# Cross-attention with image tokens: scores in two 64-row halves, six PSUM banks, and the order of the softmax around them

## The reference

```python
q = _split_heads(hidden_states @ w_q, HEADS)
k = _split_heads(text @ w_k, HEADS)
v = _split_heads(text @ w_v, HEADS)
out_text = _merge_heads(_sdpa(q, k, v))            # 56 keys
mask_ip = _ip_mask(bbox, B, S, hidden_states.dtype)
k_ip = _split_heads(ip_h @ w_k_ip, HEADS)
v_ip = _split_heads(ip_h @ w_v_ip, HEADS)
out_ip = _merge_heads(_sdpa(q, k_ip, v_ip, mask=mask_ip))   # 8 keys
out = (out_text + out_ip) @ w_out + b_out + residual
```

## Time and profile before

| | |
|---|---|
| median of 3 runs | 881.37 us |
| lowest, highest | 880.84 us, 883.45 us |
| the profiled execution | 881.16 us, of which 879.4 us are its span |
| PE busy | 874.3 us, 99% of the span, 4716 matmuls |
| PE weight loads | 752.0 us, 86%, 4716 loads |
| DVE, ACT, POOL busy | 82%, 67%, 60% |
| DMA | 21% of 16 engines' span |

### The profile page before, as it was taken

The page is one execution under the profiler, slowest core; times in us unless marked ns, Lnnn a source line. Parts: engine busy times, 40 slices in busy tenths (PEclk is TensorE's granted clock), DMA queues, the critical chain, the costliest instruction groups (busy, mean ns, idle before and its releaser), DMA issues.

```text
span 879.4 us, 13951 instructions
## 1 busy us (share of the span) xinstructions
PE 874.3 (99%) x4716; PEld 752.0 (86%) x4716; DVE 723.2 (82%) x1017; ACT 591.2 (67%) x986; POOL 524.3 (60%) x421
## 2 busy tenths in 40 slices
PE   9999999999999999999999999999999999999998
PEld 8899888888888888888888888888888888888877
DVE  6779889797888879797887879787897978888785
ACT  7766685857767585765768486675858577574773
POOL 1059677392846649293755739375664929466581
PEclk9999999999999999999999999999999999999999
DMA  9924223011030403003030301204030210301011
GB/s 315 358 100 135 83 76 127 1 68 68 1 127 1 134 0 106 21 2 132 0 127 0 134 0 37 90 0 134 0 127 0 76 58 0 119 23 39 1 48 72
DMA packets 34203, 64.63 MB, mean 73 GB/s; under 512 B 4480, under 2 KB 6784, under 8 KB 34048
## 3 DMA queue, kind: packets, MB, share of 16 engines
q1 hardware_dynamic: 33888, 62.84, 21.1%
q10 hardware_dynamic: 288, 1.44, 0.4%
HBM read 40.34 MB, written 23.59 MB: 73 GB/s over the span
## 4 chain that ended last, share of the span: by engine, by line
PE 97%; DVE 2%; POOL 1%; ACT 1%; issue 0%; POOLq 0%
PE bank L95 25%; PE bank L97 25%; PE bank L96 25%; PE bank L1131 8%; PE bank L1151 4%; PE bank L1152 4%; PE bank L1040 1%; PE bank L1046 1%; PE bank L1043 1%; DVE total L225 1%; PE bank L1061 1%; PE bank L1058 1%; PE bank L1093 0%; DVE top L219 0%; PE bank L1083 0%; POOL prob L178 0%
## 5 line engine op out<-in xcount | busy, mean ns | idle before, releaser
L512 POOL TENSOR_TENSOR oT_lo<-o_raw,oT_hi 128x512 fp32r<-128x512 f32 x78 | 101.1, 1296 | 226.0 <-ACT oT_hi L681 225.9
L178 POOL TENSOR_TENSOR prob<-prob,top 128x1120 f32<-128x1120 f32 x126 | 177.7, 1440 | 0.0
L184 POOL TENSOR_TENSOR prob<-prob,inv 128x1120 f32<-128x1120 f32 x126 | 177.2, 1441 | 0.0
L95 PE MATMUL bank<-xT_hi,wq_hi 128*128 128x512 f32 x400 | 162.9, 407 | 0.0
L919 DVE TENSOR_TENSOR o_raw<-bank,pv_part 64x512 f32<-64x512 f32 x160 | 110.2, 689 | 62.6 <-ACT pv_part L677 60.1
L95 PE MATMUL bank<-oT_hi,wo_hi 128*128 128x512 f32 (+1 forms) x405 | 157.4, 389 | 0.0
L96 PE MATMUL bank<-oT_lo,wo_hi 128*128 128x512 f32 (+1 forms) x405 | 156.7, 387 | 0.0
L97 PE MATMUL bank<-oT_hi,wo_lo 128*128 128x512 f32 (+1 forms) x405 | 156.6, 387 | 0.0
L97 PE MATMUL bank<-xT_hi,wq_lo 128*128 128x512 f32 x400 | 156.5, 391 | 0.0
L96 PE MATMUL bank<-xT_lo,wq_hi 128*128 128x512 f32 x400 | 155.9, 390 | 0.0
L677 ACT ACTIVATE pv_part<-bank 64x512 f32<-64x512 f32 x160 | 94.9, 593 | 62.7 <-PE bank L1152 60.1
(11 more groups left out here) (121 smaller groups left out, 1695.2 us busy)
## 6 DMA issues: line engine op xcount, KB each, us to landing
xin<-in_xT SPq DMA_DIRECT2D x16, 1280.0 KB, 6.8
outT<-res SPq DMA_DIRECT2D x79, 256.0 KB, 6.8
w_raw<-in_L_xattn_w_k SPq DMA_DIRECT2D x8, 320.0 KB, 5.4
w_raw<-in_L_xattn_w_k_ip SPq DMA_DIRECT2D x8, 320.0 KB, 5.8
w_raw<-in_L_xattn_w_v_ip SPq DMA_DIRECT2D x8, 320.0 KB, 3.6
w_raw<-in_L_xattn_w_v SPq DMA_DIRECT2D x8, 320.0 KB, 3.5
v_raw<-v_scratch SPq DMA_DIRECT2D x14, 140.0 KB
prob<-in_textT SPq DMA_DIRECT2D x8, 224.0 KB, 5.0
```

What stands on the lines that cost most here:

```text
L95: nc.tensor.matmul(dst, a_hi, b_hi, start=first, stop=False)
L178: ins = eng.tensor_tensor(s, s, top[:, t, n, :].unsqueeze(2).broadcast_to([P, HEADS, k1 - k0]), ALU.subtract)
L184: ins = eng.tensor_tensor(s, s, inv[:, t, n, :].unsqueeze(2).broadcast_to([P, HEADS, k1 - k0]), ALU.mult)
L512: nc.gpsimd.tensor_tensor(oT_lo[:, m, :], o_raw[:, m % 2, :], oT_hi[:, m, :].bitcast(F32), ALU.subtract).then_inc(oT_lo_done, 1)
```

## The change

The keys of a block are no longer block-diagonal over 128 rows. `k_parts` holds, for each block and part, 128 columns in which rows 0 to 63 have heads 0 and 1 and rows 64 to 127 heads 2 and 3. A step becomes six matmuls of 64 rows and 128 columns instead of three of 128 rows and 256 columns: for each of the three products one with rows 0 to 63 and one with rows 64 to 127, in turn, and into different banks. Four steps fill two banks. Scores have six banks (0 to 5) instead of four; a pair of units waits until the pair three before it is copied, and units 4 and 5 wait for the last `pv_added` of the group before. The copies read a bank as 4 by 128 columns and write them into `prob` 256 columns apart. Where a tile needed 3, 5, 8 and 10 units copied, it now needs 4, 6, 8 and 10.

The fifth remainder of the attention output goes from POOL to the head of DVE's softmax. POOL subtracts maxima 0 before mask 2 and maxima 1 before mask 3. The first transposes go tile by tile for both pairs. In the setup, `text_values` waits for all ten copies where it waited for eight.

```diff
-        k_hi, k_lo = sb("k_hi", [P, KD, HPT, KEYS], F32R), sb("k_lo", [P, KD, HPT, KEYS], F32R)
+        k_parts = sb("k_parts", [P, KD, 2, PW], F32R)
...
-        s_bank, t_bank, v_bank = bank[0:4], bank[2:4], bank[4:6]
+        s_bank, t_bank, v_bank = bank[0:6], bank[2:4], bank[4:6]
...
-            return -(-(t + 1) * SW // 512)
+            return 2 * -(-(t + 1) * KD // RUN)
...
+        def score_dst(n):
+            steps = prob[:, n // 2 * RUN * CW:(n // 2 + 1) * RUN * CW].rearrange("p (i r c) -> p r i c", r=2, c=PW)
+            return steps[:, n % 2, :, :]
...
-            for half in range(2):
-                t, m = divmod(2 * n + half, KD)
...
-                keys = [k[:, m, :, :].rearrange("p j k -> p (j k)") for k in (k_hi, k_lo)]
-                ins = three(s_bank[n % 4][:, half * CW:(half + 1) * CW], qT_hi[:, m, q_cols], qT_lo[:, m, q_cols], *keys, True, True)
-            ins.then_inc(score_ready, 1)
+            if u == 0:
+                wait(pe, score_copied, UNITS * g)
+            elif u == 1:
+                wait(pe, pT_lo_done, PAIRS * g)
+            elif u == 2:
+                wait(pe, pv_added, PAIRS * g)
+            else:
+                pe.wait_ge(score_copied, UNITS * g + 2 * u - 4)
...
+            for i in range(RUN):
+                t, m = divmod(RUN * u + i, KD)
...
+                for n, (q, part) in enumerate(((qT_hi, 0), (qT_hi, 1), (qT_lo, 0))):
+                    for r in range(2):
+                        rows = slice(r * HP, (r + 1) * HP)
+                        ins = nc.tensor.matmul(s_bank[(2 * u + r) % 6][:, i * PW:(i + 1) * PW], q[rows, m, q_cols], k_parts[rows, m, part, :], start=n == 0, stop=n == 2)
+                        if i == RUN - 1 and n == 2:
+                            ins.then_inc(score_ready, 1)
...
                 def softmax(g):
                     add_mask(pool, g, 0)
-                    oT_part(g - 1, KD - 1)
                     add_mask(pool, g, 1)
-                    add_mask(pool, g, 2)
                     for t in range(GT):
                         sub_max(pool, g, t, 1)
-                        if t == 0:
-                            add_mask(pool, g, 3)
+                        if t < 2:
+                            add_mask(pool, g, t + 2)
...
+                def last_oT_part(g):
+                    dve.wait_ge(oT_lo_done, KD * g + KD - 1)
+                    dve.wait_ge(oT_hi_done, KD * (g + 1))
+                    nc.vector.tensor_tensor(oT_lo[:, KD - 1, :], o_raw[:, (KD - 1) % 2, :], oT_hi[:, KD - 1, :].bitcast(F32), ALU.subtract).then_inc(oT_lo_done, 1)
...
-                            pe.wait_ge(score_copied, UNITS if n == 0 else UNITS - 2)
+                            pe.wait_ge(score_copied, UNITS)
...
-                    p_transpose(g, 0)
-                    p_transpose(g, 1)
+                    pe.wait_ge(score_copied, UNITS * (g + 1))
+                    for t in range(GT):
+                        pe.wait_ge(prob_done, GT * g + t + 1)
+                        for p in range(2):
+                            ins = transpose_tile(g, p, t)
+                            if t == GT - 1:
+                                ins.then_inc(pT_ready, 1)
```

More of the change, by code:

```diff
@@ L40, in attention_kernel @@
     CW = HPT * KEYS
+    PW = 2 * KEYS
+    RUN = 512 // PW
     SW = HEADS * KEYS
@@ L127, in q_lo_part, with k_head @@
             nc.vector.tensor_tensor(qT_lo[:, m, :], l_bank[(m + 1) % 2][:], qT_hi[:, m, :].bitcast(F32), ALU.subtract).then_inc(q_lo_done, 1)
-        def k_head(t, j):
-            return t[j * DH:(j + 1) * DH, :, j, :]
+        def k_head(part, j):
+            return k_parts[j * DH:(j + 1) * DH, :, part, j % 2 * KEYS:(j % 2 + 1) * KEYS]
         def k_hi_part(act, b, raw=None):
@@ L136, in k_hi_part @@
             for j in range(HPT):
-                nc.scalar.activation(k_head(k_hi, j), raw[j * DH:(j + 1) * DH], ACT.Copy).then_inc(k_hi_built, 1)
+                nc.scalar.activation(k_head(0, j), raw[j * DH:(j + 1) * DH], ACT.Copy).then_inc(k_hi_built, 1)
         def k_lo_part(dve, b, raw=None):
@@ L200, in score_unit, with copy_scores @@
                 q_cols = slice(t * P, (t + 1) * P)
[L201 to L207 removed]
+                for n, (q, part) in enumerate(((qT_hi, 0), (qT_hi, 1), (qT_lo, 0))):
[4 more added lines that the diff above has]
+                            ins.then_inc(score_ready, 1)
+        def copy_scores(act, g, n):
+            act.wait_ge(score_ready, UNITS * g + n + 1)
+            nc.scalar.activation(score_dst(n), s_bank[n % 6][:].rearrange("p (i c) -> p i c", c=PW), ACT.Copy).then_inc(score_copied, 1)
         def exponentials(act, g, t, shared):
@@ L481, in _ @@
                                         pattern=[[-1, P]], channel_multiplier=1).then_inc(ident_made, 1)
-                for buf in (k_hi, k_lo):
-                    nc.gpsimd.memset(buf[:].rearrange("p m j k -> p (m j k)").bitcast(F32), 0.0).then_inc(k_zeroed, 1)
+                nc.gpsimd.memset(k_parts[:].rearrange("p m s c -> p (m s c)").bitcast(F32), 0.0).then_inc(k_zeroed, 1)
                 mine = pool_chunks
@@ L1113, in _ @@
                         ins.then_inc(k_ipT_ready, 1)
-                for n in range(UNITS):
-                    score_unit(pe, 0, n, 0, True)
+                for u in range(UNITS // 2):
+                    score_units(pe, 0, u, 0, True)
                 for k in range(KC):
@@ L1133, in p_transpose @@
                 def p_transpose(g, p):
-                    if p < 2:
-                        pe.wait_ge(score_copied, UNITS * (g + 1))
-                    else:
-                        pe.wait_ge(pT_lo_done, PAIRS * g + p - 1)
+                    pe.wait_ge(pT_lo_done, PAIRS * g + p - 1)
                     for t in range(GT):
-                        if p == 0:
-                            pe.wait_ge(prob_done, GT * g + t + 1)
                         ins = transpose_tile(g, p, t)
@@ L1192, in scores @@
                 def scores(g, b, new_batch):
-                    for n in range(UNITS):
-                        score_unit(pe, g, n, b, new_batch)
+                    for u in range(UNITS // 2):
+                        score_units(pe, g, u, b, new_batch)
                     for m in range(KD):
@@ L1215, in last_group @@
                 def last_group(g, b):
-                    for n in range(UNITS):
-                        score_unit(pe, g, n, b, False)
+                    for u in range(UNITS // 2):
+                        score_units(pe, g, u, b, False)
                     for m in range(KD - 1):
```

18 lines of the change are left out of this document (7 added, 11 removed).

## The result

The kernel after takes 922.92 us (919.37 to 923.34) beside 881.37 us (880.84 to 883.45) before: a ratio of 1.0459, with a 95% interval of 1.0448 to 1.0470. It is 4.6% slower, and the prediction of 879.8 us was wrong; so was its whole range, which ended at 896.

What follows compares the result with a forecast made beforehand. PE, busy for 99% of the span, was taken as the bound; -8.3 (pairs) + 5.4 (passages) + 0.9 (group 0) + 0.6 (last group) = -1.4 us took the profiled 881.16 us to 879.8, range 848 to 896.

Steps and rivals of the forecast that it cites:

- The pair of halves: Score stage: the two 64-row halves load weights side by side, 0.112 us a pair, -8.3 us in all; chance 45%.
- Short loads: Score stage: the half-size matmul shortens its load too, 0.062 to 0.067 us a pair, 852 us in all; chance 27%.
- the serial rival: Score stage: only one weight load runs at a time, 0.224 us a pair, 986 us in all; chance 12%.
- The passage: Each score stage: going into and out of 64-row work costs 0.34 us, +5.4 us over 16 stages.
- Group 0 and the last group: Group 0: PE waits for all ten copies, +0.9 us; last group: subtraction 0 starts later, +0.6 us.
- Third pair of banks, unit 6, the remainder: Score stage: bank and copy waits stay hidden, the banks' with 0.7 us left; DVE's 0.7 us remainder fits its idle time.
- POOL: Middle groups' softmax: mask 0 at 4.35 us, subtraction 0 at 6.45, POOL done at 29.95, PE arriving at 30.9.
- Masks later and transposes tile by tile: Softmax and first transposes: these edits move no PE work and gain nothing while POOL has slack, put at 0.9 us.
- My sign of being wrong: PE's score stage: a length not between 6.7 and 7.8 us would show the prediction wrong.
- the sum said -1.4 us: Whole kernel: pairs -8.3, passages +5.4, group 0 +0.9 and last group +0.6 together give -1.4 us.
- The slow rivals: Score stage: loads one at a time, 986 us, 12%; or no load under its own matmul, 931 us, 7%.

## Why the prediction was wrong, point by point

- **The pair of halves.** Right. Predicted 0.112 us, the range 0.107 to 0.124. In PE of the kernel after near the end of a stage (two matmuls at a time) the pairs stand 0.11 apart, 443.50 to 443.61:

```profile
443.50 0.27 PE L214 MATMUL bank<-k_parts,qT_lo 64*128 64x128 f32 x2
443.61 0.39 PE L214 MATMUL bank<-k_parts,qT_hi 64*128 64x128 f32 x4
```

  The 60 pairs and the way out fill the 6.84 us of the stage. Short loads, the rival at 27%, is refuted by these distances (0.11, not 0.065) and by the kernel with half the columns, the serial rival by the kernel with the same rows against this one. The Trainium skill, "TensorEngine Tiling (Array Packing)", section Theoretical Speedup, gives up to 2x for a contraction of 64 rows or fewer; the stage went from 7.18 to 6.84, 1.05x.
- **The passage.** Right in kind, a little high: 0.34 us predicted, 0.3 measured. In the kernel after it is 0.10 at the entry and 0.20 at the exit (0.20 from the last pair to the first output matmul instead of 0.11, and 0.34 to the next one instead of 0.23).
- **Group 0 and the last group.** Group 0 was right in size: +0.64 us for the ten copies (+0.9 predicted). The last group cost 1.1 us, not 0.6. At its transposes PE waits 0.46 us more, as predicted, but it also waits at the third output tile, which I had not looked at: ACT moves the first tile out behind an exponential that is later (the wait for `res` by ACT, 0.4 us, in the list of the kernel with the masks as before). Against the kernel before PE loses 0.6 us there.
- **Third pair of banks, unit 6, the remainder.** Right. No wait of PE stands in the score stage. DVE does the remainder at 440.49 to 441.18, ahead of mask 0, and the kernel with it back on POOL takes the same time.
- **POOL.** The head was right: mask 0 4.36 us after the start of the scores (4.35 predicted), subtraction 0 6.54 (6.45). With the masks as before POOL ends 30.39 us after that start and PE comes at 30.81 (29.95 and 30.9 predicted).
- **"Masks later and transposes tile by tile move no work on PE and are worth nothing while POOL has slack."** This is the step that failed, by about 40 us (922.92 against 882.76); it holds for the transposes alone. I counted the slack of POOL, the engine on which the masks moved, and not of DVE, which waits for them. The number was in the earlier trace rows: DVE busy for 16.45 of 17.03 us in the output stage. DVE had 0.6 us of slack up to the first output sum; the late mask put 1.65 us of idle time ahead of it, and PE waited. The sum also had no place for the clock, which fell behind the waits and took 8 us of the 40. My sign of being wrong, a score stage outside 6.7 to 7.8 us, did not come (6.84): it looked only at the part that was right.
- **DVE's slack was used by the gain, too.** Without the late masks the sum said -1.4 us, and the kernels without them came out 1 us above the kernel before by the median. That alone is not clear of noise; the spans of the two profiled executions, 1.6 and 1.9 us longer, have the same sign. The terms that I had come out about as predicted: -6.1 (score stages) with some +1.4 (entries) and +1.5 (exits) stand for my -8.3 + 5.4, and +0.6 and +1.1 for +0.9 + 0.6, together -1.5. What lacked was in the stages behind. The output stage is 17.15 to 17.2 us instead of 17.03 (0.1 of it the passage), and in the seven groups where DVE also makes the next keys' remainders, the eight first transposes, up to the start of the query matmul behind them, take 1.2 us instead of 0.88. In the kernel with the masks as before, DVE and PE there read

```profile
448.39 4.25 DVE L145 TENSOR_TENSOR k_parts<-k_raw,k_parts 32x320 fp32r<-32x320 f32 x4
452.67 1.29 DVE L129 TENSOR_TENSOR qT_lo<-bank,qT_hi 128x512 fp32r<-128x512 f32 x2
```

```profile
453.42 0.50 PE L97 MATMUL bank<-xT_hi,wq_hi 128*128 128x512 f32 x1 [0.18 <-DVE qT_lo L129]
```

  DVE starts that `qT_lo` 24.4 us after the start of the output stage, where it was 24.0 (451.49 less 427.52) before; PE had come forward by 0.34 us and DVE had not. That is 14 x 0.05 + 7 x 0.33 = 3.0 us beside the passage, and -1.5 + 3.0 = +1.5 fits the spans. It doesn't come from the remainder that moved to DVE: the kernel with the scores alone has the same wait (1.0 us in five places) and the same 1.2 us. The wait is in the trace; no run took it away by itself.

No case of mine held the result. The slow rivals stood for mechanisms of the load path that the runs exclude; that a moved wait on POOL could hit PE by way of DVE was none of them. The six-bank halves are worth nothing that can be measured here, and no kernel that was run beats the one before.

## What to carry to other kernels

Where an instruction is moved later, follow its waiters, not its own engine: who waits for it, what stands queued behind that waiter, and how much idle time that engine has up to PE's next need. An engine at 97% in a stage has no cover to give, and a gain on PE uses up the same slack. Splitting a contraction in two halves of rows gains only what the stream exceeds the weight load; here that was 0.12 against 0.11 us, 8 us in all. The passage in and out takes 5 of them back, and the engines behind, later against PE, the rest.

## What was not expected of the hardware

- Waits of 1.8 to 2.1 us, once in a group, are followed by a fall of the granted clock to 1.2 GHz for about 3.4 us in some groups and not in others: 2 of 14 with waits of 1.8 us in one kernel, 5 of 14 in another, 10 of 14 with waits of 2.1 us, none with 0.65 or 1.0 us. The fall came 0.1 to 1.5 us behind the end of the wait.
- The clock fell also where PE waited for nothing. In the kernel with half the columns it was 0.68 in the 8.25 us shown above, with PE busy throughout, and the score stages took 7.2 to 10.2 us; in the kernel with all matmuls on rows 0 to 63 the same stages took 20.4 to 22.3 us, one of them at a mean of 0.59:

```profile
405.55:427.72 22.17, 22.17 (x122) 22.05 (x121) 7.24 (x10) 5.99 (x12) 4.02 (x6) 0.59 0.00 0
```

  The full pairs of the changed kernel ran at 1.00. A time taken from a kernel in which work was left out has to be read beside its clock.
- Two float32r loads on different halves of the rows run at the same time, in 0.11 us together; on the same rows they take 0.22.
